# Edge stream: the loops of four engines over the chunks written out, with waits for constants

## The chip, the cores and the metric

The kernel runs on one core of one Trainium2 chip. The metric is device time in microseconds: the median of 3 runs. Where a range is given, it goes from the lowest to the highest of them.

## The reference, cut to what matters

The model has an n-gram embedding, an attention, a graph layer with experts, a second attention and a routed MLP. The change lies in the graph layer. There, 262144 edges and 16384 self loops are sorted by destination in an earlier stage, and every edge needs the row of its source node:

```python
src = jnp.concatenate([edge_index[0], loops]); dst = jnp.concatenate([edge_index[1], loops])
e = leaky_relu(a_src[src] + a_dst[dst], 0.2)
e_max = segment_max(e, dst); ee = exp(e - e_max[dst])
denom = segment_sum(ee, dst); alpha = ee / (denom[dst] + 1e-16)
agg = segment_sum(h[src] * alpha[:, :, None], dst)      # per node, 4 heads x 4
...
hh = gelu(x @ W1[ei] + b1[ei]); out = out + g[..., None] * (hh @ W2[ei] + b2[ei])   # 4 experts
```

## The kernel before, in words

`edge_stream` (L765) takes the sorted list, 2176 edges on each of the 128 partitions, in 68 chunks of 32 columns. A segment's running maximum and sums are scans along the columns. A chunk goes through these engines, each with its own list of instructions, held together by semaphores alone:

- GpSimd (L860) fetches the rows of 20 of the 32 columns of a chunk, one indirect DMA a column (L877), into one of two buffers `got`. For chunk n it waits until VectorE has released the buffer that chunk n-2 had (`s_free`, L873 and L1158). From chunk 16 on it issues 2 more indirect DMAs a chunk (L867, `find`), and 3 from chunk 44 on. Its list has no loop; all its waits are for constants.
- TensorE takes the other 12 columns as 6 pairs: `pair(n, q)` (L966) is 16 matmuls of 512 columns (L975): 2 columns, 4 blocks and 2 parts of the table. They need one-hot matrices `pick`, which ScalarE makes out of row numbers that SyncE loads. The result lies in PSUM; with 6 banks and 2 a pair, pair q waits until VectorE has taken pair q-3 (`s_taken`, L970). Between the pairs TensorE computes the experts of tile pair c (`expert` L979, `output` L985), for chunks 0 to 63.
- ScalarE makes a `pick` out of 4 squares (L903) and one Relu (L905), 3 a chunk, and does the exponential of chunk c (L929), the experts' Gelu (L927, L935) and a copy (L940), with a table load between functions.
- VectorE (L1031) does, for chunk c (`turn`, L1125): the scores (L1132 to L1147), `sides` and two `take`s for chunk c+1, then the scans with the exponential (L1154 to L1160), then four more `take`s and `scores` for chunk c+1. A `take` (L1043) is 5 halvings with COPY_PREDICATED in PSUM (L1048), each of which needs the one before, and a copy (L1049). In chunks 0 to 13 a step of `listing` (L1102) stands between the scans and the third take.

TensorE, ScalarE and SyncE run chunks 0 to 63 as a loop of 32 turns of two chunks (L1025, L942, L851); VectorE has chunks 0 to 13 written out, 14 to 61 in a loop of 24 turns (L1176), and the rest written out. The values that a looped engine waits for are worked out in registers from the turn's number, and so are the addresses that go with the chunk.

Two ways of waiting stand in the code. `Chain.settle` (L91) is a bare wait before the next instruction. `pause` (L107) is a wait followed by an increment of a semaphore `s_spent` that nobody waits for:

```python
def pause(eng, sem, value, spent):
    eng.wait_ge(sem, value)
    eng.sem_inc(spent, 1)
```

`pause` is used for most waits on other engines, and in `take` also for VectorE's wait on itself after each of the 5 halvings (L1048), in the written-out chunks too.

Of the kernel before, what the change touches and what calls it, by code (L numbers as in the profile page):

```python
# [24 lines left out]
P = 128  # L25
# [53 lines left out]
class Chain:  # L79
# [4 lines left out]
    def __init__(self, eng, sem):  # L84
        self.eng, self.sem, self.base, self.n = eng, sem, 0, 0

# [4 lines left out]
    def settle(self):  # L91
        self.eng.wait_ge(self.sem, self.base + self.n)

    def turn(self, i, per_turn):
        self.start, self.per_turn = self.n if isinstance(self.base, int) else None, per_turn
        self.base, self.n = i * per_turn + self.start, 0

    def resume(self, i):

        self.base, self.n = i * self.per_turn + self.start, 0  # L100

    def end(self, turns):
        assert self.n == self.per_turn, (self.n, self.per_turn)
        self.base, self.n = 0, self.start + turns * self.per_turn


def pause(eng, sem, value, spent):  # L107

    eng.wait_ge(sem, value)
    eng.sem_inc(spent, 1)  # L110

# [37 lines left out]
PC = 12  # L149
# [615 lines left out]
def edge_stream(nc, mem, sorted_keys, table_dram, state_dram, y_dram):  # L765
# [6 lines left out]
    with ExitStack() as ctx:  # L772
# [28 lines left out]
        s_hid_p, s_hid, s_y_p, s_y, s_y_out = (sem(n) for n in ("hidp", "hid", "yp", "y", "yout"))  # L801
        s_dve, s_act, s_row0, s_diff, s_ex, s_state, s_spent, s_adr, s_adr_p, s_late, s_list, s_list_w, s_gone = (
            sem(n) for n in ("dve", "act", "row0", "diff", "ex", "state", "spent", "adr", "adrp", "late", "list", "listw", "gone"))
        s_turned_p, s_turned, s_rows, s_pick, s_got_p, s_taken = (
# [7 lines left out]
        def _(sp):  # L812
# [5 lines left out]
            def load(n, r):  # L818
                sp.dma_start(away[:, r], rows[bass.ds(n, 1), :].broadcast_to([P, 4 * P])).then_inc(s_away[r], 16)

# [12 lines left out]
            def turn(i, with_experts, loads=6):  # L833
                for r in range(2):
                    c = i * 2 + r

                    def next_load(k):
                        if r * 3 + k < loads:
                            pause(sp, s_pick, c * 3 + 6 + k, s_spent)
                            load(c * 3 + 7 + k, (r + 1 + k) % 2)  # L840

                    next_load(0)
                    pause(sp, s_state, c + 1, s_spent)
                    sp.dma_start(states[:, bass.ds(c * CH, CH), :], st[:, r, 1:, :]).then_inc(s_stored[r], 16)
                    next_load(1)
                    next_load(2)
                    if with_experts:
                        pause(sp, s_y, c + 2, s_spent)
                        sp.dma_start(y_dram.rearrange("(s t p) f -> s p t f", p=P, t=ET)[bass.ds(c, 1)].rearrange("s p t f -> (s p) t f"), y[:]).then_inc(s_y_out, 16)

            with sp.Fori(0, ESLOTS // 2) as i:  # L851
                turn(i, True)
# [39 lines left out]
        def _(act):  # L892
# [7 lines left out]
            def picks(nth, g, r, loaded):  # L900
                pause(act, s_away[r], loaded * 16, s_spent)
                for k in range(BLOCKS):
                    a.activation(pick[:, g, k], away[:, r], ACT.Square, bias=C("away")[:, k:k + 1]).then_inc(s_act, 1)  # L903
                pause(act, s_act, nth * BLOCKS, s_spent)
                a.activation(pick[:, g], pick[:, g], ACT.Relu, scale=-1.0, bias=C("ones")).then_inc(s_pick, 1)  # L905
# [7 lines left out]
            def turn(i, with_experts, count=6):  # L913
                for r in range(2):
                    c = i * 2 + r

                    def next_pick(k):
                        if r * 3 + k < count:
                            pause(act, s_got_p, c * PAIRS + 6 + 2 * k, s_spent)
                            n = r * 3 + 5 + k  # L920
                            picks(c * 3 + 6 + k, (2 + k) % PICKS, n % 2, i * 3 + n // 2 + 1)

                    next_pick(0)
                    if with_experts:
                        pause(act, s_hid_p, c * EXPERTS + 2, s_spent)
                        for n in range(2):
                            a.activation(hid[:, n], p_hid[:, n], ACT.Gelu, bias=W("e_b1")[:, n:n + 1]).then_inc(s_hid, 1)  # L927
                    pause(act, s_diff, c + 1, s_spent)
                    a.activation(ex[:], diff[:], ACT.Exp).then_inc(s_ex, 1)  # L929
                    next_pick(1)  # L930
                    if with_experts:
                        pause(act, s_hid_p, c * EXPERTS + 4, s_spent)
                        for n in range(2):
                            pause(act, s_y_p, c * EXPERTS + n + 1, s_spent)
                            a.activation(hid[:, n], p_hid[:, n], ACT.Gelu, bias=W("e_b1")[:, n + 2:n + 3]).then_inc(s_hid, 1)  # L935
                    next_pick(2)
                    if with_experts:
                        pause(act, s_y_p, c * EXPERTS + EXPERTS, s_spent)
                        pause(act, s_y_out, c * 16 + 16, s_spent)
                        a.activation(y[:], p_y[:], ACT.Copy).then_inc(s_y, 1)  # L940

            with act.Fori(0, ESLOTS // 2) as i:  # L942
                turn(i, True)
# [4 lines left out]
        def _(pe):  # L948
# [17 lines left out]
            def pair(n, q, first=False):  # L966
                if q % 2 == 0:
                    pause(pe, s_pick, n * PICKS + q // 2 + 1, s_spent)
                if not (first and q < BANKS // 2):
                    pause(pe, s_taken, n * PAIRS + q - BANKS // 2 + 1, s_spent)  # L970
                for c in range(2):
# [7 lines left out]
            def expert(c, n):  # L979
                both = xts[:, bass.ds(c, 1)].rearrange("p one n -> p (one n)")  # L980
                for t in range(ET):
                    mm = pe.matmul(p_hid[:, n % 2, t * P:t * P + P], W("e_w1_odd" if t else "e_w1")[:, n * HID:n * HID + HID], both, start=True, stop=True)  # L982
                mm.then_inc(s_hid_p, 1)

            def output(c, n):  # L985
                pause(pe, s_hid, c * EXPERTS + n + 1, s_spent)
                for t in range(ET):
# [9 lines left out]
            def turn(i, with_experts, pairs=2):  # L997
                for r in range(2):
# [9 lines left out]
                    if with_experts:  # L1008
                        pause(pe, s_y, c + 1, s_spent)
                        for t in range(ET):  # L1010
# [13 lines left out]

            with pe.Fori(0, ESLOTS // 2) as i:  # L1025
                turn(i, True)
# [4 lines left out]
        def _(dve):  # L1031
# [8 lines left out]
            def sides(n):  # L1040
                ch.step(v.tensor_tensor(bits[:], spread(side[:, bass.ds(n, 1), :].rearrange("p n c -> p (n c)"), SIDE_BITS), repeat(powers[:], PC), ALU.bitwise_and)); ch.settle()

            def take(n, r, q):  # L1043
                pause(dve, s_got_p, n * PAIRS + q + 1, s_spent)
                at = p_got[:, 2 * q % BANKS:2 * q % BANKS + 2]
                for b in range(SIDE_BITS - 1, -1, -1):
                    half = 16 << b
                    ch.step(v.copy_predicated(at[:, :, 0:half], spread(bits[:, 2 * q:2 * q + 2, b], half), at[:, :, half:2 * half])); pause(dve, s_dve, ch.base + ch.n, s_spent)  # L1048
                ch.step(v.tensor_copy(got[:, r, GC + 2 * q:GC + 2 * q + 2, 0:16], at[:, :, 0:16])); ch.settle()  # L1049
# [75 lines left out]
            def turn(i, takes=2, listings=None):  # L1125
                for r in range(2):
                    c = i * 2 + r
                    cols = bass.ds(c * CH, CH)
                    pause(dve, s_landed[r], (i + 1) * (16 * GC), s_spent)
                    g = got[:, r]  # L1130
# [6 lines left out]
                    ch.step(v.scalar_tensor_tensor(out=e[:], in0=e[:], scalar=0.2, in1=e[:], op0=ALU.mult, op1=ALU.max)); ch.settle()  # L1137
                    pause(dve, s_stored[r], (i + 1) * 16, s_spent)
                    ch.step(v.tensor_copy(st[:, r, 0, :], st[:, 1 - r, CH, :]))
# [8 lines left out]
                    if r < takes:  # L1148
                        sides(c + 1)
                        for q in range(0, 2):  # L1150
                            take(c + 1, 1 - r, q)
                    pause(dve, s_ex, c + 1, s_spent)
                    for k in range(4):
# [17 lines left out]
            for i in range(LISTED):  # L1171
                turn(i, listings=2 * i)
            PER = 2 * (38 + 1 + (SIDE_BITS + 1) * PAIRS + 4)
            TURNS = CHUNKS // 2
            LOOPED = ESLOTS // 2 - 1 - LISTED
            with dve.Fori(0, LOOPED) as i:  # L1176
                ch.turn(i, PER)
                turn(i + LISTED)
            ch.resume(LOOPED)
            turn(ESLOTS // 2 - 1)  # L1180
            ch.resume(LOOPED + 1)
            turn(ESLOTS // 2)
            ch.end(LOOPED + 2)
            turn(TURNS - 1, 1)
# [759 lines left out]
```

## Time and profile before

| | us |
|---|---|
| median of 3 runs | 3511.93 |
| lowest, highest | 3511.32, 3512.47 |
| the profiled execution's own time | 3511.03 |
| its span | 3509.2 |
| edge stream: first L1132 of chunk 0 | 795.45 |
| edge stream: last L1132, chunk 67 | 2968.07 |

L1132 is the first VectorE instruction of a chunk, so the distance between two of them is the time of a chunk. In the views, an instruction's idle time is what its engine stood still just before it, and behind the arrow stands what ended that. "issue" means that nothing in the trace was waited for. Instructions that only wait, count or branch are no busy time.

### The profile page before, as it was taken

The page shows a single profiled execution, that of the slowest core. Times are in us where ns is not written, and L with a number is a line of the kernel's source. Part 1 is how long each engine was busy: PE and PEld are TensorE (multiplying, and loading weights), DVE is VectorE, ACT ScalarE, POOL GpSimd, SP SyncE. Part 2 cuts the span into 40 slices and gives each one's busy share as a digit, 9 for nine tenths or more (in the row PEclk, how much of TensorE's full clock was granted, in tenths as well). Part 3 has the DMA queues.
Part 4 walks back from the last instruction along what each step waited for, and adds up shares of the span by engine and source line. Part 5 has one row for each costly group of instructions (what it writes and reads, how often), then busy time and mean ns, then how long its engine had stood idle before and what let it go on. Part 6 is the DMA issues. An engine that isn't in the chain of part 4 may idle for free. (4 is left out here: it accounts for less than half of the span.)

```text
span 3509.2 us, 50874 instructions
## 1 busy us (share of the span) xinstructions
PE 2667.1 (76%) x12450; PEld 2118.4 (60%) x12450; DVE 2626.0 (75%) x7198; ACT 2117.0 (60%) x4084; POOL 2121.5 (60%) x2073
## 2 busy tenths in 40 slices
PE   1666566658888898898888988888988896177773
PEld 1545455446676777677777767777777774044452
DVE  8987888847777776776776766666667777789975
ACT  2666666655565656665666566566656662178884
POOL 7877775036656566666666666766666674745410
PEclk8677777769898999999999999999999998578896
DMA  2111111022222222222221222222222221311102
GB/s 74 23 26 25 25 26 20 2 57 47 54 43 54 50 57 58 54 44 58 54 57 45 58 55 44 58 54 49 52 58 55 49 53 36 103 29 53 28 1 48
DMA packets 172983, 161.27 MB, mean 46 GB/s; under 512 B 73128, under 2 KB 130888, under 8 KB 172104
## 3 DMA queue, kind: packets, MB, share of 16 engines
q1 hardware_dynamic: 108512, 127.47, 11.9%
q0 software_dynamic: 64240, 31.62, 7.8%
q14 instruction: 196, 1.61, 0.2%
q8 instruction: 35, 0.57, 0.1%
HBM read 107.49 MB, written 51.45 MB: 45 GB/s over the span
## 5 line engine op out<-in xcount | busy, mean ns | idle before, releaser
L975 PE MATMUL es_pgot<-parts,es_pick 128*128 128x512 f32 x6528 | 1648.1, 413 | 268.7 <-DVEq L1050 265.4
L877 POOL DMA_INDIRECT es_got<-node_table,late x1360 | 1318.2, 969 | 717.0 <-issue 380.7
L975 PEld LDWEIGHTS es_pgot<-parts,es_pick 128*128 128x128 f32 x6528 | 1294.3, 201 | 558.8 <-issue 284.0
L1048 DVE COPY_PREDICATED es_pgot<-es_bits,es_pgot 128x512 f32<-128x512 int32 (+4 forms) x2040 | 753.3, 369 | 381.8 <-DVE es_got L1049 74.2
L903 ACT ACTIVATE es_pick<-es_away,consts 128x512 fp32r<-128x512 f32 x816 | 521.5, 711 | 284.6 <-PE es_pgot L975 277.2
L299 POOL DMA_INDIRECT fr_ring<-in_emb,fr_rows x384 | 462.6, 1205 | 132.2 <-issue 116.4
L905 ACT ACTIVATE es_pick<-es_pick,consts 128x2048 fp32r<-128x2048 f32 x204 | 409.3, 2007 | 24.2
L1160 DVE TENSOR_TENSOR_SCAN es_st<-es_ex,es_st,es_msg 128x32 f32<-128x32 f32 x1088 | 209.9, 282 | 10.0
L515 DVE TENSOR_TENSOR fr_space<-fr_space 128x1024 f32<-128x1024 f32 x173 | 211.6, 1223 | 5.5 <-DVE fr_space L516 2.4
L516 DVE TENSOR_TENSOR fr_space<-fr_space 128x1024 f32<-128x1024 f32 x173 | 211.1, 1220 | 0.0
L903 ACT ACT_TABLE_LOAD x32 | 41.1, 1283 | 224.0 <-PE es_pgot L975 224.0
L929 ACT ACT_TABLE_LOAD x65 | 83.4, 1283 | 139.5 <-DVE es_diff L1147 139.0
L1409 POOL DMA_INDIRECT bk_ring<-edge_states,node_end x128 | 136.1, 1063 | 38.3 <-issue 32.8
L867 POOL DMA_INDIRECT es_gone<-sorted_keys,es_atnode x128 | 121.7, 950 | 39.0 <-issue 39.0
L988 PEld LDWEIGHTS ex_py<-weights,ex_hid 128*128 128x128 f32 x1024 | 129.0, 191 | 26.6 <-issue 21.2
L982 PE MATMUL ex_phid<-xc,weights 128*128 x1024 | 138.3, 278 | 0.0
L988 PE MATMUL ex_py<-weights,ex_hid 128*128 128x64 f32 x1024 | 134.7, 275 | 0.0
L982 PEld LDWEIGHTS ex_phid<-xc,weights 128*128 128x128 f32 x1024 | 129.3, 192 | 5.0
L1049 DVE COPY es_got<-es_pgot 128x32 f32<-128x32 f32 x408 | 78.3, 192 | 70.4 <-DVE es_pgot L1048 17.9
L927 ACT ACTIVATE ex_hid<-ex_phid,weights 128x256 f32<-128x256 f32 x128 | 53.7, 471 | 106.3 <-PE ex_phid L982 106.0
L701 PE MATMUL fr_pa<-consts,fr_x 128*128 128x128 f32 x64 | 20.8, 427 | 126.8 <-DVE fr_x L463 126.7
L1425 POOL TENSOR_TENSOR h<-h,bk_x 128x256 f32<-128x256 f32 x32 | 36.8, 1150 | 123.4 <-DVE bk_x L1689 123.3
(366 smaller groups left out, 4025.3 us busy)
## 6 DMA issues: line engine op xcount, KB each, us to landing
es_away<-sorted_keys SPq DMA_DIRECT2D x204, 256.0 KB
edge_states<-es_st SPq DMA_DIRECT2D x68, 384.0 KB
es_got<-node_table,late POOLq DMA_INDIRECT x1360
expert_outputs<-ex_y SPq DMA_DIRECT2D x64, 256.0 KB
bk_y<-expert_outputs SPq DMA_DIRECT2D x8, 2048.0 KB, 8.4
fr_ring<-in_emb,fr_rows POOLq DMA_INDIRECT x384, 2.5
out_dram<-h SPq DMA_DIRECT2D x4, 1024.0 KB, 5.1
late<-in_edges SPq DMA_DIRECT2D x1, 2048.0 KB, 9.2
```

The costliest lines, as they stand in the source:

```text
L299: pool.indirect_dma_start(out=ring[:, r, n, t, :], out_offset=None, in_=tables[n], in_offset=bass.IndirectOffsetOnAxis(ap=rows[:, s * ST + ...
L515: ch.step(v.tensor_tensor(o[:, :, 0, :], left, right, ALU.min))
L516: ch.step(v.tensor_tensor(o[:, :, 1, :], left, right, ALU.max))
L877: pool.indirect_dma_start(out=got[:, r, k, :], out_offset=None, in_=table_dram, in_offset=bass.IndirectOffsetOnAxis(ap=src[:, n, k:k + 1]. ...
L903: a.activation(pick[:, g, k], away[:, r], ACT.Square, bias=C("away")[:, k:k + 1]).then_inc(s_act, 1)
L905: a.activation(pick[:, g], pick[:, g], ACT.Relu, scale=-1.0, bias=C("ones")).then_inc(s_pick, 1)
L975: mm = pe.matmul(p_got[:, (2 * q + c) % BANKS], pick[:, q // 2, k, at * P:at * P + P], parts[:, part, k], start=(k == 0 and part == 0), st ...
L982: mm = pe.matmul(p_hid[:, n % 2, t * P:t * P + P], W("e_w1_odd" if t else "e_w1")[:, n * HID:n * HID + HID], both, start=True, stop=True)
L988: mm = pe.matmul(p_y[:, t, n * D:n * D + D], hid[:, n % 2, t * P:t * P + P], W("e_w2")[:, n * D:n * D + D], start=False, stop=True, skip_g ...
L1048: ch.step(v.copy_predicated(at[:, :, 0:half], spread(bits[:, 2 * q:2 * q + 2, b], half), at[:, :, half:2 * half])); pause(dve, s_dve, ch.b ...
L1160: ch.step(v.tensor_tensor_scan(st[:, r, 1:, 8 + j], ex[:, 0, :, j // 4], msg[:, :, j], st[:, r, 0, 8 + j:9 + j], ALU.mult, ALU.add))
L1409: pool.indirect_dma_start(out=ring[:, g % 2, t, :], out_offset=None, in_=state_dram, in_offset=bass.IndirectOffsetOnAxis(ap=mem["node_end" ...
```

## The change

Every loop over the chunks in `edge_stream` becomes a Python loop that writes each turn out. All wait values and addresses are constants. `pause` and `s_spent` are gone: each `pause` is now a bare wait. In `take`, the pause after each halving becomes `settle`. `Chain` loses what it needed for loops. Order, operations, buffers and data of all engines stay the same; GpSimd's list is not touched. The core of the diff (the same edit at every `pause` and every register address is left out):

```diff
     def settle(self):
-        self.eng.wait_ge(self.sem, self.base + self.n)
...
-def pause(eng, sem, value, spent):
-
-    eng.wait_ge(sem, value)
-    eng.sem_inc(spent, 1)
+        self.eng.wait_ge(self.sem, self.n)
...
-            with sp.Fori(0, ESLOTS // 2) as i:
+            for i in range(ESLOTS // 2):
                 turn(i, True)
...
-                pause(act, s_away[r], loaded * 16, s_spent)
+                act.wait_ge(s_away[r], loaded * 16)
...
-            with act.Fori(0, ESLOTS // 2) as i:
+            for i in range(ESLOTS // 2):
                 turn(i, True)
...
-                    pause(pe, s_taken, n * PAIRS + q - BANKS // 2 + 1, s_spent)
+                    pe.wait_ge(s_taken, n * PAIRS + q - BANKS // 2 + 1)
...
-            with pe.Fori(0, ESLOTS // 2) as i:
+            for i in range(ESLOTS // 2):
                 turn(i, True)
...
             def take(n, r, q):
-                pause(dve, s_got_p, n * PAIRS + q + 1, s_spent)
+                dve.wait_ge(s_got_p, n * PAIRS + q + 1)
...
-                    ch.step(v.copy_predicated(at[:, :, 0:half], spread(bits[:, 2 * q:2 * q + 2, b], half), at[:, :, half:2 * half])); pause(dve, s_dve, ch.base + ch.n, s_spent)
+                    ch.step(v.copy_predicated(at[:, :, 0:half], spread(bits[:, 2 * q:2 * q + 2, b], half), at[:, :, half:2 * half])); ch.settle()
...
-                    pause(dve, s_landed[r], (i + 1) * (16 * GC), s_spent)
+                    dve.wait_ge(s_landed[r], (i + 1) * (16 * GC))
...
-                    pause(dve, s_stored[r], (i + 1) * 16, s_spent)
+                    dve.wait_ge(s_stored[r], (i + 1) * 16)
...
-                    pause(dve, s_ex, c + 1, s_spent)
+                    dve.wait_ge(s_ex, c + 1)
...
-            PER = 2 * (38 + 1 + (SIDE_BITS + 1) * PAIRS + 4)
             TURNS = CHUNKS // 2
-            LOOPED = ESLOTS // 2 - 1 - LISTED
-            with dve.Fori(0, LOOPED) as i:
-                ch.turn(i, PER)
-                turn(i + LISTED)
-            ch.resume(LOOPED)
-            turn(ESLOTS // 2 - 1)
-            ch.resume(LOOPED + 1)
-            turn(ESLOTS // 2)
-            ch.end(LOOPED + 2)
+            for i in range(LISTED, TURNS - 1):
+                turn(i)
             turn(TURNS - 1, 1)
```

## Rows read from the trace of the kernel before

**Rows 1.** Windows: us, then busy us (and instructions) of PE, PEld, DVE, ACT, POOL; PEclk, DMA.
```profile
797.00:1275.00 478.00, 407.03 (x1854) 334.48 (x1853) 373.92 (x1178) 279.73 (x337) 288.98 (x282) 0.90 0.23 50
1275.00:2822.00 1547.00, 1373.77 (x6354) 1127.06 (x6354) 1073.88 (x3845) 959.71 (x1155) 1023.98 (x1075) 0.94 0.23 54
```
**Rows 2.** Timeline of VectorE: the starts of chunks 0, 14, 30, 31, 32, 55 and 67.
```profile
795.45 0.47 DVE L1132 TENSOR_TENSOR es_aself<-es_got,late 128x128 f32<-128x128 f32 x1 [0.17 <-DVE es_got L1057]
...
1273.37 0.47 DVE L1132 TENSOR_TENSOR es_aself<-es_got,late 128x128 f32<-128x128 f32 x1 [0.48 <-DVE es_got L1057]
...
1790.04 0.47 DVE L1132 TENSOR_TENSOR es_aself<-es_got,late 128x128 f32<-128x128 f32 x1 [3.24 <-issue]
...
1820.12 0.47 DVE L1132 TENSOR_TENSOR es_aself<-es_got,late 128x128 f32<-128x128 f32 x1 [0.29 <-DVE es_got L1057]
...
1854.12 0.47 DVE L1132 TENSOR_TENSOR es_aself<-es_got,late 128x128 f32<-128x128 f32 x1 [3.61 <-issue]
...
2596.41 0.47 DVE L1132 TENSOR_TENSOR es_aself<-es_got,late 128x128 f32<-128x128 f32 x1 [0.29 <-DVE es_got L1057]
...
2968.07 0.47 DVE L1132 TENSOR_TENSOR es_aself<-es_got,late 128x128 f32<-128x128 f32 x1 [0.18 <-DVE es_got L1057]
```
**Rows 3.** Waits, chunks 14 to 61: who waited for what, us, times, longest.
```profile
POOL es_got L877 <- DVEq L1158: 201.2, 46, 6.8
PE es_pgot L975 <- DVEq L1050: 168.2, 80, 4.5
DVE es_aself L1132 <- issue: 87.5, 23, 4.5
DVE es_pgot L1048 <- PE es_pgot L975: 14.5, 26, 0.9
```
**Rows 4.** Lines by shape, VectorE, 1275 to 2822 us: busy us, mean ns | idle us before.
```profile
L1048 DVE COPY_PREDICATED es_pgot<-es_bits,es_pgot 128x256 f32<-128x256 int32 x288 | 123.6, 429 | 41.9
...
L1136 DVE TENSOR_TENSOR es_e<-es_got,es_adst 128x128 f32<-128x128 f32 x49 | 23.0, 470 | 1.7
L1137 DVE SCALAR_TENSOR_TENSOR es_e<-es_e 128x128 f32<-128x128 f32 x49 | 14.4, 294 | 1.7
```
**Rows 5.** Timeline of VectorE, looped: two takes, and the start of the scores.
```profile
1806.36 2.43 DVE L1048 COPY_PREDICATED es_pgot<-es_bits,es_pgot 128x512 f32<-128x512 int32 x5 [0.34 <-DVE es_st L1160]
...
1809.45 2.43 DVE L1048 COPY_PREDICATED es_pgot<-es_bits,es_pgot 128x512 f32<-128x512 int32 x5 [0.33 <-DVE es_got L1049]
...
1822.56 0.38 DVE L1139 COPY es_st<-es_st 128x24 f32<-128x24 f32 x1 [0.17 <-DVE es_e L1137]
```
**Rows 6.** Timeline of VectorE, written out, chunk 63: a take.
```profile
2868.41 2.43 DVE L1048 COPY_PREDICATED es_pgot<-es_bits,es_pgot 128x512 f32<-128x512 int32 x5 [0.26 <-DVE es_got L1049]
```
**Rows 7.** Lines of GpSimd, 1275 to 2822 us.
```profile
L877 POOL DMA_INDIRECT es_got<-node_table,late x961 | 916.8, 954 | 488.6 <-issue 266.4 <-DVEq L1158 209.1 <-PE es_pgot L975 13.1
L867 POOL DMA_INDIRECT es_gone<-sorted_keys,es_atnode x113 | 107.5, 951 | 34.4 <-issue 34.4
```
**Rows 8.** Timeline of GpSimd, chunk 57: the first two and last gathers, the next chunk's first.
```profile
2609.84 0.94 POOL L877 DMA_INDIRECT es_got<-node_table,late  x1 [1.89 <-DVEq L1158]
2611.09 1.04 POOL L877 DMA_INDIRECT es_got<-node_table,late  x1 [0.30 <-issue]
...
2637.57 0.94 POOL L867 DMA_INDIRECT es_gone<-sorted_keys,es_atnode  x1 [0.30 <-issue]
2643.90 0.94 POOL L877 DMA_INDIRECT es_got<-node_table,late  x1 [5.39 <-DVEq L1158]
```
**Rows 9.** Timeline of TensorE, turn of chunk 6: one whole turn and its wait.
```profile
1006.02 1.05 PE L982 MATMUL ex_phid<-xc,weights 128*128 x8
...
1013.51 7.54 PE L975 MATMUL es_pgot<-parts,es_pick 128*128 128x512 f32 x32
1020.89 1.00 PE L988 MATMUL ex_py<-weights,ex_hid 128*128 128x64 f32 x8
1026.99 13.33 PE L975 MATMUL es_pgot<-parts,es_pick 128*128 128x512 f32 x48 [5.10 <-DVEq L1050]
1040.16 1.05 PE L982 MATMUL ex_phid<-xc,weights 128*128 x8
```
**Rows 10.** Waits of VectorE, chunks 1 to 12 (written out).
```profile
DVE es_pgot L1048 <- PE es_pgot L975: 4.4, 12, 0.7
...
DVE es_pgot L1048 <- DVE es_pgot L1048: 1.2, 3, 0.5
```
**Rows 11.** The page's groups: the indirect DMAs of the stage before, beside the sort.
```profile
L299 POOL DMA_INDIRECT fr_ring<-in_emb,fr_rows x384 | 462.6, 1205 | 132.2 <-issue 116.4
```

More of the change, by code:

```diff
@@ L84, in __init__ @@
     def __init__(self, eng, sem):
-        self.eng, self.sem, self.base, self.n = eng, sem, 0, 0
+        self.eng, self.sem, self.n = eng, sem, 0
     def step(self, ins):
@@ L91, in settle @@
     def settle(self):
-        self.eng.wait_ge(self.sem, self.base + self.n)
[L94 to L104, printed above, removed]
-def pause(eng, sem, value, spent):
-    eng.wait_ge(sem, value)
-    eng.sem_inc(spent, 1)
+        self.eng.wait_ge(self.sem, self.n)
 def spread(ap, n):
@@ L801, in edge_stream @@
         s_hid_p, s_hid, s_y_p, s_y, s_y_out = (sem(n) for n in ("hidp", "hid", "yp", "y", "yout"))
-        s_dve, s_act, s_row0, s_diff, s_ex, s_state, s_spent, s_adr, s_adr_p, s_late, s_list, s_list_w, s_gone = (
-            sem(n) for n in ("dve", "act", "row0", "diff", "ex", "state", "spent", "adr", "adrp", "late", "list", "listw", "gone"))
+        s_dve, s_act, s_row0, s_diff, s_ex, s_state, s_adr, s_adr_p, s_late, s_list, s_list_w, s_gone = (
+            sem(n) for n in ("dve", "act", "row0", "diff", "ex", "state", "adr", "adrp", "late", "list", "listw", "gone"))
         s_turned_p, s_turned, s_rows, s_pick, s_got_p, s_taken = (
@@ L818, in load @@
             def load(n, r):
-                sp.dma_start(away[:, r], rows[bass.ds(n, 1), :].broadcast_to([P, 4 * P])).then_inc(s_away[r], 16)
+                sp.dma_start(away[:, r], rows[n:n + 1, :].broadcast_to([P, 4 * P])).then_inc(s_away[r], 16)
             sp.wait_ge(s_turned, 2)
@@ L838, in next_load @@
                         if r * 3 + k < loads:
-                            pause(sp, s_pick, c * 3 + 6 + k, s_spent)
+                            sp.wait_ge(s_pick, c * 3 + 6 + k)
                             load(c * 3 + 7 + k, (r + 1 + k) % 2)
                     next_load(0)
-                    pause(sp, s_state, c + 1, s_spent)
+                    sp.wait_ge(s_state, c + 1)
                     sp.dma_start(states[:, bass.ds(c * CH, CH), :], st[:, r, 1:, :]).then_inc(s_stored[r], 16)
@@ L847, in turn @@
                     if with_experts:
-                        pause(sp, s_y, c + 2, s_spent)
-                        sp.dma_start(y_dram.rearrange("(s t p) f -> s p t f", p=P, t=ET)[bass.ds(c, 1)].rearrange("s p t f -> (s p) t f"), y[:]).then_inc(s_y_out, 16)
-            with sp.Fori(0, ESLOTS // 2) as i:
+                        sp.wait_ge(s_y, c + 2)
+                        sp.dma_start(y_dram.rearrange("(s t p) f -> s p t f", p=P, t=ET)[c:c + 1].rearrange("s p t f -> (s p) t f"), y[:]).then_inc(s_y_out, 16)
+            for i in range(ESLOTS // 2):
                 turn(i, True)
@@ L900, in picks @@
             def picks(nth, g, r, loaded):
-                pause(act, s_away[r], loaded * 16, s_spent)
+                act.wait_ge(s_away[r], loaded * 16)
                 for k in range(BLOCKS):
                     a.activation(pick[:, g, k], away[:, r], ACT.Square, bias=C("away")[:, k:k + 1]).then_inc(s_act, 1)
-                pause(act, s_act, nth * BLOCKS, s_spent)
+                act.wait_ge(s_act, nth * BLOCKS)
                 a.activation(pick[:, g], pick[:, g], ACT.Relu, scale=-1.0, bias=C("ones")).then_inc(s_pick, 1)
@@ L918, in next_pick @@
                         if r * 3 + k < count:
-                            pause(act, s_got_p, c * PAIRS + 6 + 2 * k, s_spent)
+                            act.wait_ge(s_got_p, c * PAIRS + 6 + 2 * k)
                             n = r * 3 + 5 + k
@@ L924, in turn @@
                     if with_experts:
-                        pause(act, s_hid_p, c * EXPERTS + 2, s_spent)
+                        act.wait_ge(s_hid_p, c * EXPERTS + 2)
                         for n in range(2):
                             a.activation(hid[:, n], p_hid[:, n], ACT.Gelu, bias=W("e_b1")[:, n:n + 1]).then_inc(s_hid, 1)
-                    pause(act, s_diff, c + 1, s_spent)
+                    act.wait_ge(s_diff, c + 1)
                     a.activation(ex[:], diff[:], ACT.Exp).then_inc(s_ex, 1)
@@ L931, in turn @@
                     if with_experts:
-                        pause(act, s_hid_p, c * EXPERTS + 4, s_spent)
+                        act.wait_ge(s_hid_p, c * EXPERTS + 4)
                         for n in range(2):
-                            pause(act, s_y_p, c * EXPERTS + n + 1, s_spent)
+                            act.wait_ge(s_y_p, c * EXPERTS + n + 1)
                             a.activation(hid[:, n], p_hid[:, n], ACT.Gelu, bias=W("e_b1")[:, n + 2:n + 3]).then_inc(s_hid, 1)
@@ L937, in turn @@
                     if with_experts:
-                        pause(act, s_y_p, c * EXPERTS + EXPERTS, s_spent)
-                        pause(act, s_y_out, c * 16 + 16, s_spent)
+                        act.wait_ge(s_y_p, c * EXPERTS + EXPERTS)
+                        act.wait_ge(s_y_out, c * 16 + 16)
                         a.activation(y[:], p_y[:], ACT.Copy).then_inc(s_y, 1)
-            with act.Fori(0, ESLOTS // 2) as i:
+            for i in range(ESLOTS // 2):
                 turn(i, True)
@@ L967, in pair @@
                 if q % 2 == 0:
-                    pause(pe, s_pick, n * PICKS + q // 2 + 1, s_spent)
+                    pe.wait_ge(s_pick, n * PICKS + q // 2 + 1)
                 if not (first and q < BANKS // 2):
-                    pause(pe, s_taken, n * PAIRS + q - BANKS // 2 + 1, s_spent)
+                    pe.wait_ge(s_taken, n * PAIRS + q - BANKS // 2 + 1)
                 for c in range(2):
@@ L979, in expert @@
             def expert(c, n):
-                both = xts[:, bass.ds(c, 1)].rearrange("p one n -> p (one n)")
+                both = xts[:, c:c + 1].rearrange("p one n -> p (one n)")
                 for t in range(ET):
@@ L985, in output @@
             def output(c, n):
-                pause(pe, s_hid, c * EXPERTS + n + 1, s_spent)
+                pe.wait_ge(s_hid, c * EXPERTS + n + 1)
                 for t in range(ET):
@@ L1008, in turn @@
                     if with_experts:
-                        pause(pe, s_y, c + 1, s_spent)
+                        pe.wait_ge(s_y, c + 1)
                         for t in range(ET):
@@ L1040, in sides @@
             def sides(n):
-                ch.step(v.tensor_tensor(bits[:], spread(side[:, bass.ds(n, 1), :].rearrange("p n c -> p (n c)"), SIDE_BITS), repeat(powers[:], PC), ALU.bitwise_and)); ch.settle()
+                ch.step(v.tensor_tensor(bits[:], spread(side[:, n:n + 1, :].rearrange("p n c -> p (n c)"), SIDE_BITS), repeat(powers[:], PC), ALU.bitwise_and)); ch.settle()
             def take(n, r, q):
-                pause(dve, s_got_p, n * PAIRS + q + 1, s_spent)
+                dve.wait_ge(s_got_p, n * PAIRS + q + 1)
                 at = p_got[:, 2 * q % BANKS:2 * q % BANKS + 2]
```

## The prediction

> **What bounds the kernel now.** First the windows by stage [rows 1]. No engine is full in the edge stream: from 1275 to 2822 us TensorE is busy 89%, VectorE 69%, ScalarE 62%, GpSimd 66%. So the bound is a chain, or an engine whose time is not counted as busy. The waits tell which [rows 3]. TensorE waits 168 us for VectorE's takes and GpSimd 201 us for a buffer that VectorE releases, while VectorE waits 14.5 us for TensorE. VectorE is the bound, and the 31% in which it is not busy are gaps of its own. The chunk starts [rows 2] show two kinds: chunk 30 to 31 takes 1820.12 - 1790.04 = 30.1 us, chunk 31 to 32 takes 34.0. The longer one ends at the loop's jump back, where VectorE stands 3.61 us for nothing that the trace shows; in all 87.5 us in 23 turns [rows 3].
>
> The stage's two stretches: A, chunks 0 to 14, 1273.37 - 795.45 = 477.9 us, 34.1 a chunk (VectorE written out, with the listing in each chunk). B, chunks 14 to 67, 2968.07 - 1273.37 = 1694.7 us, 32.0 a chunk.
>
> **VectorE's part of the change.** Inside a take each halving waits for the one before. Through `pause`, the idle time is 41.9/288 = 0.146 us [rows 4]. Where VectorE waits for itself with the bare `settle`, as before L1136 and L1137, it is 1.7/49 = 0.035. All 5 pauses after halvings become `settle`: 0.111 us each, 5 x 6 takes = 30 a chunk, 3.3 us. I take the 0.035 although those rows are SBUF operations and the halvings are in PSUM; the ends of this step are 0 and 3.3 us.
>
> Between takes stand an increment (kept), a register operation in the loop, and the pause: 0.33 us looped [rows 5], 0.26 written out [rows 6]. With pause and register gone I expect what one semaphore instruction costs, 0.146. That is 0.19 on 5 takes a chunk looped, 0.95 us, or 0.11, 0.55 us, written out. The other pauses (before L1132, L1139, the first take and L1154) and the registers of the addresses: 0.29 before L1132 looped and 0.17 written out [rows 2], 0.17 before L1139 [rows 5]; taken to 0.035 each, and 0.26 to 0.146 before the scans, together 0.5 us written out and about 1.0 looped. If a double wait keeps an instruction of its own, 0.1 x 3 of it stays.
>
> So VectorE alone needs 30.1 - 5.2 = 24.9 us a chunk in B with no jump back, and 34.1 - 4.4 = 29.7 in A, where the listing stays.
>
> **What is late next.** VectorE's gain only counts until another engine binds.
>
> TensorE: its turn from 1006.02 to 1040.16 is 34.14 us [rows 9], of which 5.10 are its wait for a take. After that wait 48 matmuls need 13.17 us until the next group; 32 clean ones need 7.38 before, so 48 would need 11.07. The 2.1 us between are a granted clock of half, 1.2 instead of 2.4 GHz, after the idle time. TensorE itself needs 34.14 - 5.10 - 2.1 = 26.9 us a chunk. Its own pauses lie under running matmuls; I cost them at nothing, at most 8 x 0.1 us if the cover goes.
>
> GpSimd: an indirect DMA takes 0.954 us and is followed by 34.4/113 = 0.304 in which it waits for nothing, 1.258 together [rows 7]. The change does not touch it. A chunk has 20, from chunk 16 on 22 (27.7 us), from 44 on 23 (28.9 us). That is above 26.9 and 24.9. GpSimd has some lead now and waits for the buffer (5.39 us ahead of chunk 58) [rows 8]; once the others are quicker, this wait goes and nothing is left to give.
>
> **ScalarE and SyncE**: busy 960 us in 48 chunks, 20 a chunk [rows 1], with most waits for TensorE; a `pick` is needed a good half chunk after its buffer is free. I cost their loops at nothing: the cover is at least 5 us a chunk, and GpSimd is above them.
>
> **The sum.** Stretch A: VectorE binds, 20 x 1.258 = 25.2 for GpSimd. But the takes get quicker than the pairs. The sixth pair may start only when the third take is done; it then needs 16 x 0.23 = 3.7 us, up to 2 more at the low clock, while VectorE does two takes in 4.7. The wait there, 4.4 us in 12 chunks now [rows 10], should grow by about 0.7 a chunk (0 to 1.3). 14 x (4.4 - 0.7) = 52 us; ends 43 and 62.
>
> Stretch B: GpSimd starts the gathers of chunk 16 when chunk 14's buffer is released. That is 2609.84 - 2596.41 = 13.4 us after a chunk's start now [rows 2, 8], and with the two takes in between quicker by 0.75 us each and 0.6 off around them 11.3. From there it works without a break: chunks 16 to 66 are 51 x 20 gathers, chunk 67 another 20, and before those 28 x 2 + 23 x 3 = 125 searches, 1165 DMAs x 1.258 = 1466 us. Some 3 us later the last rows have landed and chunk 67 starts: 11.3 + 1466 + 3 = 1480 us, against 1694.7. That is 215 us less. The first dozen chunks of B go at TensorE's 26.9; GpSimd's lead of some 14 us is used up by chunk 30, and it does not change the end.
>
> Before chunk 0 and after chunk 67: 12 takes' pauses less, 2 us.
>
> 52 + 215 + 2 = 269, off the profiled execution's 3511.0 us: 3242. The median is 0.9 above it, 3243. I forecast 3244, with 1 us more for written-out code's own small stalls: VectorE shows three of up to 0.5 us in 12 written-out chunks [rows 10].
>
> A rule on the jump back. The row first: 3.61 us of idle time where the shorter form of the same step has 0.29 [rows 2]. The Trainium skill, Runtime: NRT & Kernel Launch, section on instruction fetch mechanics, says that a taken branch to code out of the fetch window forces a fetch, and that straight code is fetched ahead, mostly hidden. The trace agrees with both halves; the second speaks against the rival of fetch stalls below.
>
> **Rivals.**
>
> 1. TensorE stays in the way: each GpSimd-bound chunk leaves it 2 us idle, it falls to the low clock for the next pair, its pair comes late to the take, and the release of the buffer slips. For it: 8 to 12 slow matmuls follow waits of 2 to 5 us. Against: GpSimd does not wait for a buffer any more then, and TensorE needs 26.9 + 2.1 = 29.0 where GpSimd needs 28.9, so it costs little. If it cost 1.5 us a chunk in all of B: 53 x 1.5 = 80, 3324 us.
>
> 2. The waits do not get cheaper, only the loop goes. Then VectorE keeps its 30.1 less the register operations, 29.6 a chunk in B, and nothing in A: 53 x (32.0 - 29.6) = 127, 3385 us. For it: no row shows a bare wait between PSUM operations. Against: the pause's semaphore instruction is what is seen in the gap, and bare waits are 0.035 throughout.
>
> 3. The other side, slower: GpSimd is held by VectorE. Beside the sort, the same indirect DMA takes 1.205 us instead of 0.954 [rows 11], and in the edge stream single ones take 1.04 [rows 8]. If a denser VectorE brings the mean to 1.205 here, a DMA costs 1.51, and since GpSimd is the new bound all of it counts: 1165 x 0.25 = 291, 3244 + 291 = 3535 us. It turns slower from 1.19 us on. Against: the number of VectorE operations in a chunk stays, only gaps between them go, and at 69% busy the mean is 10 ns above the undisturbed 0.944.
> The Trainium skill, SBUF — State Buffer, section on the two separate sides, has a rule for it: GpSimd can't write the descriptors of its DMAs while VectorE runs an operation of a two-port mode. By that rule the 0.25 us hang on the kind of operation and not on how dense they are, which is the sum's side.
>
> 4. Written-out code must be fetched without end. If TensorE paid the jump's 3.3 us once a chunk, with the low clock behind it, its turn would be 26.9 + 3.3 + 2.1 = 32.3: no gain in B, 14 x 1.8 = 25 in A, 3486 us. Against: VectorE's three short stalls in 12 written-out chunks [rows 10].
>
> 5. A little better: no growing wait in A (-10), DMAs at 1.245 in B (-14): 3220 us.
>
> **How the numbers follow.** Forecast, with case 5 in its neighbourhood: 0.77 (3220 to 3265). Rival 1: 0.12. Rival 2: 0.05. Rival 3: 0.03. Rival 4: 0.03. The range must reach over most of rival 1 and below case 5: 3218 to 3310. What can be told from no change is 0.2%, 7 us; no case lies there but where rivals 3 and 4 end a few us from 3512. Faster 0.96, same 0.01, slower 0.03.
>
> **What would show it.** Right: halvings at 0.035 us idle; no issue wait before L1132; VectorE's waits for TensorE or landed rows now longer than its own gaps; GpSimd's wait for L1158 gone from chunk 17 on, and chunks of 27.7 and 28.9 us in B; chunks of 30.4 in A. Wrong: an idle time of 0.1 or more between halvings (rival 2), indirect DMAs over 1.0 us in the mean (rival 3), issue waits of over 1 us on TensorE (rival 4), chunks above 29.5 us in B while GpSimd waits for L1158 (rival 1). The forecast fails low if the 0.30 us between GpSimd's DMAs shrinks, for which I see no reason.

## The result, and the profile after

The changed kernel takes 3271.6 us (median of 4 runs, 3269.7 to 3273.6). The kernel before takes 3511.6 over the 4 runs it is held against (3509.4 to 3512.5). The ratio is 0.9318 with a 95% interval of 0.9304 to 0.9332: 240 us less. Forecast were 3244 us, with a range of 3218 to 3310. Beside the later runs the kernel before took 3512 to 3514 us.

First the chunk starts on VectorE after the change (chunks 0, 14 and 67), to be held against [rows 2]:

```profile
800.26 0.47 DVE L1114 TENSOR_TENSOR es_aself<-es_got,late 128x128 f32<-128x128 f32 x1
...
1218.07 0.47 DVE L1114 TENSOR_TENSOR es_aself<-es_got,late 128x128 f32<-128x128 f32 x1
...
2729.69 0.47 DVE L1114 TENSOR_TENSOR es_aself<-es_got,late 128x128 f32<-128x128 f32 x1 [4.77 <-DMA es_got<-node_table,late]
```

| | before | forecast | after |
|---|---|---|---|
| stretch A, chunks 0 to 14 | 477.9 | 426 | 417.8 |
| stretch B, chunks 14 to 67 | 1694.7 | 1480 | 1511.6 |
| start of chunk 0 | 795.4 | 794 | 800.3 |
| rest after chunk 67 starts | 541.1 | 540 | 541.5 |

The forecast's 2 us outside the two stretches are split evenly in this table. The start of chunk 0 lies between 795.4 and 801.7 us in all profiles of this study, and kernels that differ from each other only behind it lie up to 4 us apart there, so its 5 us are not put down to the change.

The lines by shape of VectorE from 1218 to 2730 us show the idle time between halvings, to be held against [rows 4]:

```profile
L1030 DVE COPY_PREDICATED es_pgot<-es_bits,es_pgot 128x256 f32<-128x256 int32 x318 | 136.2, 428 | 10.9
```

That is 10.9/318 = 0.034 us instead of 0.146. A take's timeline:

```profile
1940.06 1.98 DVE L1030 COPY_PREDICATED es_pgot<-es_bits,es_pgot 128x512 f32<-128x512 int32 x5
...
1942.40 1.98 DVE L1030 COPY_PREDICATED es_pgot<-es_bits,es_pgot 128x512 f32<-128x512 int32 x5
```

The five halvings need 1.98 us instead of 2.43, and takes follow each other by 2.34 us instead of 3.09 [rows 5].

The waits in B (1218 to 2730 us) have turned round, against [rows 3]:

```profile
DVE es_aself L1114 <- DMA es_got<-node_table,late: 171.1, 41, 6.1
DVE es_pgot L1030 <- PE es_pgot L957: 27.0, 14, 2.1
...
POOL es_got L859 <- issue: 318.7, 1041, 1.0
...
POOL es_got L859 <- DVEq L1140: 0.3, 1, 0.3
```

VectorE no longer stands for "issue" at a chunk's start but waits for gathered rows, 171 us in 41 chunks; GpSimd's wait for a released buffer has gone from 201 us to 0.3. And the windows (busy us and instructions of PE, PEld, DVE, ACT, POOL, then clock and DMA), against [rows 1]:

```profile
800.00:1218.00 418.00, 391.14 (x1853) 322.28 (x1852) 373.30 (x1178) 264.52 (x324) 287.86 (x280) 0.96 0.26 57
1218.00:1565.00 347.00, 347.00 (x1719) 288.62 (x1718) 289.72 (x1043) 243.99 (x300) 264.10 (x274) 1.00 0.29 66
1218.00:1900.00 682.00, 668.44 (x3290) 553.71 (x3289) 554.64 (x1994) 464.93 (x574) 518.88 (x533) 1.00 0.28 63
1900.00:2730.00 830.00, 752.79 (x3581) 617.28 (x3579) 627.48 (x2249) 498.61 (x612) 633.56 (x645) 0.98 0.25 56
```

Until 1565 us TensorE is busy all the time at the full granted clock: chunks 15 to 25 take 26.7 us each. From chunk 27 on, which starts there, chunks take 28 to 29 us and from chunk 45 on 29 to 30 (single ones 25.9 and 30.8), and TensorE has idle time again: it is busy 96% up to 1900 us and 91% behind it.

What the forecast did not have is in GpSimd's lines (1218 to 2730 us), against [rows 7]:

```profile
L859 POOL DMA_INDIRECT es_got<-node_table,late x1049 | 1029.9, 982 | 321.2 <-issue 318.7 <-PE es_pgot L957 2.1 <-DVEq L1140 0.3
L849 POOL DMA_INDIRECT es_gone<-sorted_keys,es_atnode x127 | 123.5, 972 | 38.7 <-issue 38.7
```

The mean DMA is 0.981 us instead of 0.954; times 1165 that is 31 us, all of stretch B's miss. The median is 0.944 in both kernels, so it is not that every DMA is a little longer: in B, 43 DMAs take over 1.3 us, the longest 1.82, where none took over 1.14 before.

### The profile page after: what moved, and what is told of

Same layout as the page of the kernel before. It is cut to its first block and busy times, and to the rows that moved or that the text cites. A ratio compares the mean times of both kernels' runs of the same rounds, so it can differ in the third digit from the quotient of the medians.

```text
span 3271.2 us, 41047 instructions
## 1 busy us (share of the span) xinstructions
PE 2583.2 (79%) x12450; PEld 2057.2 (63%) x12450; DVE 2621.7 (80%) x7198; ACT 2036.4 (62%) x4021; POOL 2157.4 (66%) x2073
## 5 line engine op out<-in xcount | busy, mean ns | idle before, releaser
L859 POOL DMA_INDIRECT es_got<-node_table,late x1360 | 1347.1, 991 | 461.1 <-issue 408.6
L957 PE MATMUL es_pgot<-parts,es_pick 128*128 128x512 f32 x6528 | 1562.0, 397 | 111.6 <-DVEq L1032 107.5
L957 PEld LDWEIGHTS es_pgot<-parts,es_pick 128*128 128x128 f32 x6528 | 1229.5, 191 | 377.4 <-DVEq L1032 122.0
L498 DVE TENSOR_TENSOR fr_space<-fr_space 128x1024 f32<-128x1024 f32 x173 | 210.7, 1218 | 0.0
L1114 DVE TENSOR_TENSOR es_aself<-es_got,late 128x128 f32<-128x128 f32 x68 | 31.9, 470 | 172.0 <-DMA es_got<-node_table,late 171.1
L964 PE MATMUL ex_phid<-xc,weights 128*128 128x128 f32 x1024 | 138.3, 278 | 0.0
L911 ACT ACTIVATE es_ex<-es_diff 128x256 f32<-128x256 f32 x68 | 28.4, 417 | 146.7 <-DVE es_diff L1129 146.4
L660 PE MATMUL fr_turned<-fr_ring,consts 128*128 128x128 f32 x384 | 63.0, 328 | 55.7 <-DMA fr_ring<-in_emb,fr_rows 55.7
```

What stands on the lines that cost most here:

```text
L498: ch.step(v.tensor_tensor(o[:, :, 1, :], left, right, ALU.max))
L859: pool.indirect_dma_start(out=got[:, r, k, :], out_offset=None, in_=table_dram, in_offset=bass.IndirectOffsetOnAxis(ap=src[:, n, k:k + 1]. ...
L957: mm = pe.matmul(p_got[:, (2 * q + c) % BANKS], pick[:, q // 2, k, at * P:at * P + P], parts[:, part, k], start=(k == 0 and part == 0), st ...
```

## The experiments

**Which part of the change brings what.** First, only the loops (all four engines; every pause kept):

```diff
-            with dve.Fori(0, LOOPED) as i:
-                ch.turn(i, PER)
-                turn(i + LISTED)
+            for i in range(LISTED, TURNS - 1):
+                turn(i)
```


> All loops written out, every pause kept. Theory (VectorE's own gaps bound both stretches before; the loop costs its jump back and register operations, the pauses cost the semaphore instruction between dependent halvings): VectorE needs 29.6 us a chunk in stretch B, as in the last five written-out chunks of the kernel before, against 32.0; stretch A stays at 478. B: 53 x 29.6 = 1569 instead of 1695, total about 3386 us. Rival (only the bare waits matter, the jump back is hidden elsewhere): 3500 or more. Rival (written-out code is what brings the gain and the pauses cost nothing): near 3272.

It measured 3382.1 us (3380.5 to 3388.3). Stretch A took 477.5 us and B 1562.6, nearly all its chunks 29.2 to 29.6 us (single ones up to 30.4). GpSimd still waited 82 us in B for buffers that VectorE releases:

```profile
POOL es_got L877 <- DVEq L1158: 82.2, 52, 5.0
```

So the loops are worth 130 us, all in B.

Then the changed kernel, with one pause back:

```diff
-half:2 * half])); ch.settle()
+half:2 * half])); pause(dve, s_dve, ch.n, s_spent)
```


> The changed kernel, but with the pause after each halving in take back. Theory: 30 x 0.11 = 3.3 us a chunk return to VectorE. Stretch A is bound by VectorE and gets 14 x 3 = 42 us longer (418 to 460). In B VectorE needs 28.2, just below GpSimd's 28 to 29.5, so B gets only some 10 us longer: total about 3325. Rival (VectorE still binds in B): 67 x 3.3 = 221 more, 3493. Rival (the halvings' waits do not matter): 3272.

It measured 3324.7 us (3323.7 to 3325.5). A took 468.9 us and B 1513.6: 51 us come back in A and 2 in B, where chunks 14 to 58 take 28.1 to 28.8 us instead of first 26.7 and then 28 to 30. VectorE's 3.3 us a chunk cost next to nothing where GpSimd binds in the end. In part that is a balance: GpSimd waited 23 us for buffers here, but its mean DMA in B was 0.969 us instead of 0.981, which is 13 us less. Taken out in this order, the loops are worth 130 us, the pauses outside the halvings 3382 - 3325 = 57, and the halving pauses 53.

Last, VectorE alone; TensorE, ScalarE and SyncE as before:

```diff
             with pe.Fori(0, ESLOTS // 2) as i:      # unchanged, as with act and sp
...
-            with dve.Fori(0, LOOPED) as i:
+            for i in range(LISTED, TURNS - 1):
...
-                pause(dve, s_got_p, n * PAIRS + q + 1, s_spent)
+                dve.wait_ge(s_got_p, n * PAIRS + q + 1)
```


> Only VectorE's loop is written out and only its pauses are bare waits; TensorE, ScalarE and SyncE keep loops, registers and pauses. Theory: the whole gain is VectorE's, total 3272 within 8 us. Rival (the loops of the others count once VectorE is quicker): TensorE's pauses and jumps add 0.1 to 1 us to each chunk in the 28 chunks in which it binds and in A, total 3285 to 3330.

It measured 3265.3 us (3263.2 to 3265.8), 6 us less than the full change. The chunks that TensorE binds take 26.7 us here too. The other three engines' part of the change is worth nothing. The 6 us that it even cost lie in GpSimd's DMAs: their mean in B was 0.973 here and 0.981 there, which is worth 9 us, and B was 10 us shorter. Why more of them were long there was not settled.

**What binds after it.** The changed kernel without the searches:

```diff
-                    find(count)
...
-            ch.step(v.scalar_tensor_tensor(out=mem["node_end"][:], in0=gone[:], scalar=-1.0, ...
+            ch.step(v.memset(mem["node_end"][:], 0))
```


> The changed kernel without the 128 indirect DMAs that look up where the nodes end; the later stage then reads row 0 for every node. Theory (GpSimd binds B from about chunk 28 on): it needs 20 x 1.286 = 25.7 us a chunk, below TensorE's 26.7, so TensorE binds all of B: 53 x 26.8 = 1420 instead of 1512, total about 3181, and VectorE's waits for landed rows vanish. Rival (TensorE falls to the low clock and the chain between it and VectorE makes the 28 to 29.5 us): B stays within 20 us of 1512, total 3255 to 3273.

It measured 3174.1 us (3173.2 to 3174.7). B took 1408.5 us; from chunk 15 to 63 nearly every chunk takes 26.7 us. Its waits in B:

```profile
DVE es_pgot L1029 <- PE es_pgot L956: 99.2, 50, 2.1
POOL es_got L859 <- DVEq L1139: 88.6, 51, 1.9
```

VectorE waits for TensorE, GpSimd again for a buffer, nobody for gathered rows. Leaving out GpSimd's 125 DMAs in B saves 103 us. So GpSimd was the bound and TensorE the next one. TensorE is busy 99% of B here at a granted clock of 1.00, so in the changed kernel its lower clock was a result of the waiting and not its cause (rival 1 falls).

**Why GpSimd's DMAs got longer.** In the timeline of the changed kernel, all 43 long ones lie in VectorE's stream of products and scans. 22 start between 0.12 us before the first product of a chunk and 0.30 behind it, the other 21 about 1 us into the 16 scans that follow. One of the first kind:

```profile
1359.20 0.95 POOL L859 DMA_INDIRECT es_got<-node_table,late  x1 [0.30 <-issue]
1359.82 0.86 DVE L1136 TENSOR_TENSOR_SCAN es_st<-es_ex,es_st 128x32 f32<-128x32 f32 x4
1360.46 1.82 POOL L859 DMA_INDIRECT es_got<-node_table,late  x1 [0.30 <-issue]
1360.58 0.88 DVE L1138 TENSOR_TENSOR es_msg<-es_got,es_ex 128x128 f32<-128x128 f32 x4
```

Before, GpSimd stood waiting for the buffer while the products ran, since they are what the release waits for: in B not one of its DMAs started between 0.3 us before the first product and 0.7 behind it. After, 48 do, and 38 of them take over 1.1 us. Of the 31 us that B's DMAs took longer in all, 20 are theirs and 9 those of DMAs beside the scans. The kernel without the searches is a check on this. Its VectorE streams are as unbroken as in the changed kernel, but GpSimd waits for buffers again, and its DMAs are as short as before (1250 to 2600 us):

```profile
L859 POOL DMA_INDIRECT es_got<-node_table,late x1014 | 968.9, 956 | 381.9 <-issue 293.2 <-DVEq L1139 88.1 <-PE es_pgot L956 0.6
```

Two kernels add VectorE operations without waits between them: more products, and, as a control, copies out of PSUM.

```diff
-                    for k in range(4):
-                        ch.step(v.tensor_tensor(msg[:, :, 4 * k:4 * k + 4], ...
+                    for to in (msg, more[0], more[1]):
+                        for k in range(4):
+                            ch.step(v.tensor_tensor(to[:, :, 4 * k:4 * k + 4], ...
```


> The changed kernel with the message products of each chunk computed three times, the second and third into tiles nobody reads: 8 more VectorE operations with two SBUF inputs, 1.6 us a chunk, without a wait between them. Theory (in the changed kernel GpSimd's DMAs are held while VectorE streams products and scans without a pause; that is the 0.027 us by which their mean in stretch B rose, 31 us in all): A +22 us (VectorE binds); in B VectorE stays below GpSimd, but the stream is 5.5 instead of 3.9 us, the mean DMA rises from 0.981 to 0.995 to 1.03 us and B by 15 to 60 us: total 3310 to 3355. Rival (the longer DMAs have another reason, as the denser traffic): B within 8 us of 1512, total 3295.

It measured 3386.2 us (3384.1 to 3394.5), with A at 448.4 and B at 1592.8. The direction was right, the size was not: A grew by 31 us instead of 22, and B by 81 instead of 15 to 60. Two chunks of its timeline show why:

```profile
1308.94 0.88 DVE L1140 TENSOR_TENSOR es_msg<-es_got,es_ex 128x128 f32<-128x128 f32 x4
1309.05 3.21 POOL L860 DMA_INDIRECT es_got<-node_table,late  x1 [0.30 <-issue]
1309.74 1.70 DVE L1140 TENSOR_TENSOR es_more<-es_got,es_ex 128x128 f32<-128x128 f32 x8
...
1335.24 3.40 POOL L860 DMA_INDIRECT es_got<-node_table,late  x1 [0.30 <-issue]
1335.32 0.88 DVE L1140 TENSOR_TENSOR es_msg<-es_got,es_ex 128x128 f32<-128x128 f32 x4
1336.12 1.70 DVE L1140 TENSOR_TENSOR es_more<-es_got,es_ex 128x128 f32<-128x128 f32 x8
```

Started 0.11 us after the first product or 0.08 before it, the DMA ends 3.32 us after that product started: with the stream, not after its own length. All of B says the same. 52 of the 53 DMAs that started up to 1.1 us behind the first product or 0.3 before it ended 3.31 to 3.33 us after it; in the changed kernel, where the products run 0.88 us and not 2.50, the 38 long ones ended after 1.69 to 1.71. Both are 0.8 us behind the end of the last product. The scans hold less: the 24 DMAs over 1.1 us that start within the 16 scans of the changed kernel end 2.3 to 2.7 us after the first scan, while the scans go on to 3.1.

```diff
+                if q == 1:
+                    for n8 in range(8):
+                        ch.step(v.tensor_copy(more[:, n8], at[:, :, 0:16]))
```


> The control to the tripled products: 8 more copies from PSUM into a tile nobody reads in the second take of each chunk, also 1 to 1.8 us of VectorE time without a wait, but with one PSUM input each. Theory (held by two SBUF inputs): mean DMA stays at 0.98 us, B within 10 us of 1512, only A grows by 14 to 25 us: total 3286 to 3300. Rival (any dense VectorE work holds GpSimd): mean DMA and B grow as in the tripled products. Rival (VectorE binds B): B +53 x 1.5 = 80 us.

It measured 3274.7 us (3272.5 to 3276.0), with A at 433.2 and B at 1501.6. These are as many operations more; A is 15 us longer and B 10 shorter. The 8 copies run in 0.87 us, as long as the 4 products of a chunk, and none of the 74 DMAs beside them in B took over 0.95 us. GpSimd's lines of both, 1250 to 2600 us:

```profile
L860 POOL DMA_INDIRECT es_got<-node_table,late x891 | 944.7, 1060 | 273.8 <-issue 266.1 <-PE es_pgot L958 5.8 <-DVEq L1142 1.9
```
```profile
L860 POOL DMA_INDIRECT es_got<-node_table,late x945 | 917.0, 970 | 290.5 <-issue 285.1 <-PE es_pgot L958 5.5
```

The mean is 1.060 us with the products and 0.970 with the copies. That is even below the 0.981 of the changed kernel, as it was with VectorE alone written out (0.973): fewer DMAs happened to fall on the products and were held, 26 over 1.1 us with the copies against 38. Then the test in the other direction: the changed kernel with waits of VectorE on itself in the streams, from chunk 14 on.

```diff
+                        if c >= 14 and k == 1:
+                            ch.settle()                # after two products
...
+                    if c >= 14:
+                        ch.settle()                    # after the first four scans
...
+                        if c >= 14 and j % 3 == 2:
+                            ch.settle()                # after every third scan
```


> The changed kernel with waits of VectorE on itself put into its streams of products and scans from chunk 14 on: after the first four scans, after two products, after every third of the sixteen scans. Theory (GpSimd is held while operations with two SBUF inputs follow each other without a gap): the mean DMA in B falls from 0.981 to about 0.955, B from 1512 to about 1482, while VectorE's added 0.13 us each, 1 us a chunk, stays below GpSimd's 28 to 29: total 3243. Rival (it is the number of such operations and not their density): mean DMA stays 0.98, total 3272 to 3285.

It measured 3242.9 us (3242.0 to 3246.3), with B at 1481.2. Its line (1250 to 2600 us):

```profile
L859 POOL DMA_INDIRECT es_got<-node_table,late x955 | 912.7, 956 | 291.3 <-issue 287.0 <-PE es_pgot L957 4.3
```

The mean is back at 0.956 us, and the 30 us that the forecast missed in B are back. 51 DMAs started beside the products here, and none took over 1.1 us. That the hold is by density and kind together is shown by these three. What in the kind matters is not: products and copies differ in where their inputs lie, in their number of inputs and in size. Nor do the runs show which resource is held. The Trainium skill, SBUF — State Buffer, section on the two separate sides, names one, a port pair shared by VectorE and GpSimd: a VectorE operation of a two-port mode locks it for the whole instruction, one with two SBUF inputs only against a GpSimd operation that reads SBUF, and `tensor_tensor` is said not to have stalled DMAs. The runs agree that the kind of operation decides. They differ in that products, which are `tensor_tensor` with both inputs in SBUF, did hold GpSimd's DMAs, up to 3.44 us, and in that the hold outlasts one instruction: it goes on as long as the products follow each other without a wait.

**A version that beats both.** More buffers for gathered rows (here 3; four is the same with 4 and 2):

```diff
-        got = sb("es_got", [P, 2, CH, ROW], F32)
+        got = sb("es_got", [P, 3, CH, ROW], F32)
...
-                        pool.wait_ge(s_got_p, min(n, CHUNKS - 1) * PAIRS - 4 + k // 4)
+                        pool.wait_ge(s_got_p, (min(n, CHUNKS - 1) - 1) * PAIRS - 4 + k // 4)
```


> The changed kernel with three instead of two buffers for gathered rows, and GpSimd's waits for TensorE one chunk looser. Theory (GpSimd binds the end of B and has 30.3 - 25.2 = 5 us a chunk to spare in A, which it cannot bank with two buffers): it enters B one chunk of 27 us further ahead, B 1512 - 27 = 1485, total 3246. Rival (TensorE or the chain binds): no change, 3272. Rival (gathers further ahead collide more with VectorE's streams): gain under 10 us.

It measured 3237.8 us (3236.0 to 3242.3), with B at 1479.1. TensorE binds up to chunk 43 (26.7 us a chunk), then GpSimd. Of B's 33 us some 10 come from the mean DMA, 0.973 instead of 0.981 us; only the rest is the lead.

> Four buffers, GpSimd's waits for TensorE two chunks looser. Theory: two chunks of lead, B 1458, total 3219; TensorE's 26.7 us a chunk (1415 for B) is not reached yet. Rivals as with three buffers: 3272, or a gain under 20 us.

It measured 3239.6 us (3235.4 to 3248.5): no gain over three. GpSimd's waits from 757 to 1300 us say where it went:

```profile
POOL sorted_keys L865 <- DVEq L1107: 30.1, 1, 30.1
```

GpSimd, far ahead, stands waiting for the listing; with three buffers this wait was 8.1 us. The next kernel moves what needs the listing to later chunks:

```diff
-LIST_AT = 15
+LIST_AT = 17
...
-                    count = 2 if n < CHUNKS - 24 else 3
+                    count = 2 if n < CHUNKS - 28 else 3
```


> Four buffers, with the listing's store and the searches two chunks later (from chunk 18, 2 a chunk up to 39, then 3). Theory (with four buffers GpSimd had run ahead in A, and then stood 30.1 us before chunk 16 for VectorE's listing, which threw the fourth buffer's lead away): that wait vanishes, and B is 1480 - 26 = 1454, total 3214. Rival (the fourth buffer's lead is bounded by something else, as the waits for TensorE): no change against 3239.

It measured 3208.3 us (3204.9 to 3209.9), with B at 1447.7, and the wait for the listing is gone. And with the broken streams:

> Both: four buffers with the later searches, and the broken streams. Theory: the gains add until TensorE's 26.7 us a chunk bind all of B: 53 x 26.7 = 1415 at the least, 1454 - 28 = 1426 by the sum; total 3186. Rival (VectorE's added microsecond delays TensorE's pairs where TensorE binds): B 10 to 50 us longer than that.

It measured 3199.0 us (3198.4 to 3203.2), 0.9112 (0.9097 to 0.9128) of the kernel before, the fastest here that does all the work. B is 1439.4, 13 us more than the 1426 that were expected and 22 more than the two measured gains together would give (1511.6 - 63.9 - 30.4 = 1417.3). Part of this is that the gains overlap. With four buffers the mean DMA was already 0.971 and not 0.981, and breaking the streams brought it to 0.961: 11 us, not 30. The rest was not separated.

## Why the prediction was right, and where its size was off

- *VectorE's own gaps bind, not its work.* This is shown: removing the loop and the pauses on VectorE alone gives the whole gain.
- *A halving's wait falls from 0.146 to 0.035.* Measured 0.034, in PSUM as in SBUF; rival 2 falls. *Takes 0.19 us closer besides:* 3.09 to 2.34 us, 0.75 in all, where the steps gave 0.55 + 0.19 = 0.74.
- *The jump back costs 3.6 us, and written-out code nothing like it.* With the loops out alone, nearly all of B's chunks were 29.2 to 29.6 us; 29.6 was expected. Rival 4 falls: TensorE has 26.7 us a chunk in written-out code too.
- *Stretch A: 29.7 us plus 0.7 of waiting for TensorE.* Measured 417.8 instead of 426. The waiting term was too large: with shorter idle time TensorE spent less time at the low clock (granted 0.96 instead of 0.90; that this is the reason is argued, not tested), and VectorE waited 7.5 us in 12 chunks for it, 0.6 a chunk in all and 0.25 more than before, not 0.7 more.
- *TensorE 26.9 us a chunk, GpSimd above it.* TensorE measured 26.7, and without the searches it binds nearly all of B. GpSimd's lead was used up at chunk 27; the prediction had said a dozen chunks of B, and chunk 30 at the latest.
- *1165 DMAs of 1.258 us make B.* This is the term that was mis-sized: they took 1.286 (0.981 and 0.305 until the next). The rival for the slower side had the mechanism, GpSimd held by VectorE, and its argument against it (the operations of a chunk stay the same, only gaps go) was wrong in one point: it was not asked where in the chunk GpSimd used to stand still. It stood beside the products that hold it most, and the change removed that very wait. Its other argument, that the hold hangs on the kind of operation and not on how dense they are, was wrong too: the same operations with waits between them brought the mean from 0.981 to 0.956. The price was 0.027 us a DMA, a tenth of the rival's 0.25.
- *ScalarE's, SyncE's and TensorE's loops cost nothing:* this is shown, within 6 us.
- *The total.* In the profiled execution B was 32 us longer than forecast, A 8 shorter, and the start of chunk 0 came 6 later, which nothing in the change explains. That the total is within 28 us thus owes 8 us to an error the other way.

## What to carry to other kernels

When an engine looks 70% busy and everyone waits for it, sum its idle times by line: 0.11 us too much at each of 30 halvings a chunk, some more at the other pauses, and 3.6 us at each jump back came to 240 us here. Before removing a wait, work out the next engine's time with its issue gaps (1.258 us for a DMA shown as 0.954), and look at what runs beside the place where that engine used to wait. An engine that binds late but stands idle early can bank its lead only in buffers, and any wait in its list (here the listing's) can throw it away.

## What the runs showed of the hardware that was not expected

- An indirect DMA of GpSimd that starts beside a stream of VectorE products ends 0.8 us after the last of them, however long they are at it: up to 3.4 us instead of 0.94. Beside the 16 scans it takes up to 1.6 us, but ends before they do. Beside copies out of PSUM it takes 0.95 at most. A wait of VectorE on itself after every second product and every third scan is enough to let it through: no DMA beside the products took over 1.1 us then.
- On VectorE, between halvings of which each needs the one before, a wait followed by an increment of an unused semaphore leaves 0.146 us of idle time and the bare wait 0.034. On TensorE and ScalarE the same pauses cost nothing that the total shows (3265 us with them and their loops, 3272 without).
